# One 128x512 product expands a group of 512 edges in the head and scatter stage: windows of 16 rows for each tile, offsets for four groups in one load

## The chip, the cores and the metric

One core of one Trainium2 chip runs the whole program. The metric is the device time of one launch in microseconds. Lower is better.

## What is computed

Four graph layers run one after the other on 3125 nodes with 128 features and 53125 edges, which are sorted by their destination. Only the third and the fourth matter here. N, D, H, Dh are 3125, 128, 8, 16.

```python
# layer 3 (x, k, q, v: one row for each node)
kw = jnp.einsum('ehd,hdo->eho', k[src], rel_att)
a = jnp.einsum('eho,eho->eh', kw, q[dst]) * rel_pri * inv_sqrt_d
m = jnp.einsum('ehd,hdo->eho', v[src], rel_msg)
attn = softmax of a over the edges of one dst
h_agg = jax.ops.segment_sum(m * attn[..., None], dst, num_segments=N)
...
# layer 4: rows = src, cols = dst
gathered = vals[:, None] * x[cols]
side = jax.ops.segment_sum(gathered, rows, num_segments=n)
```

Layer 3 needs the row q[dst] for each edge, and layer 4 the row x[dst]. Both are got by expansion: since the edges are sorted by dst, a short window of node rows holds all that a group of edges needs, and a product with a matrix of ones and zeros copies each row to its edges. With the inputs of this case the 512 edges of any group span at most 35 nodes, and the 128 edges of any tile at most 11, which was counted from dst.

## The kernel before

Edges are cut into Q = 104 groups of GE = 512, and each group into J = 4 tiles of 128. Every layer makes a pass over the 104 groups. The stage that changes is `head_and_rows`, and it makes two such passes, which overlap by two groups. The head pass (layer 3) works on kv rows gathered by src and on rows of `q_table`. The rows pass (layer 4) works on rows of `x_last`, multiplies them by the edge's weight and scatters them by src order. `number[rows, q]` numbers the 208 expansions of the two passes from 0, and n below is that number.

One expansion takes these steps, each on its own queue:

- **SP** (`load`): reads the group's first node from `base_sb` into a register (L419), loads the offsets of the 512 edges from that node, broadcast to 64 partitions (L2003, 128 KB written, waits for `spread_made` of two expansions ago), and then loads the window, 64 node rows to 64 partitions (L2013, 32 KB, waits for `expanded` of expansion n - 3, since there are WS = 3 window slots).
- **ACT** (`spread_out`): spread = relu(1 - |offset - lane|) in two operations on 64x512 (L2196, L2198). This is the 0/1 matrix. It waits for `expanded` of expansion n - 2.
- **PE** (`expand`): four products of 64 rows, one for each tile of 128 edges, into the 128x512 buffer `ps_q[n % 2]` (L2059). It waits for the window, the spread, and `taken` of expansion n - 2.
- **DVE**: `score` (L2335) in the head pass or `weigh_row` (L2273) in the rows pass takes `ps_q`, and sends `taken`.
- **POOL**: in the head pass, four indirect DMAs for each group gather kv rows (L1971). Group q waits for `expanded` to reach q - 4. In the rows pass, four indirect DMAs for each group scatter the weighed rows (L1985), after `taken` of this group and `expanded` of the next one.

The order on each engine is written out: `turns` gives the turns, and in turn t every engine runs its part of group t, with the softmax of a chunk of 13 groups (`links` on SP: 16 loads, L1995; `maxima`, `sums`, `shares` on DVE), the summing up of the head pass (`total_up`, L2095) and in the rows pass the counting that gives each row its place (`count` on PE, L2072 to L2074; `mark` and `place` on DVE) between the expansions. PE's instructions are executed in that order, so are SP's and ACT's.

The first layer's pass (`rel` tables, L703 to L780) already works by tiles: there the windows of a group are four loads of 64 rows (L722), one for each tile, with the bases of the four tiles read at once (`window_bases`). The set-up of the changed stage on DVE (L2553 to L2565) ends with the semaphore `set_up`, for which ACT waits before its first spread.

Of the kernel before, what the change touches and what calls it, by code (L numbers as in the profile page):

```python
# [26 lines left out]
P = 128  # L27
N = 3125
D = 128
# [37 lines left out]
def build(nc, x, src, dst, edge_attr_64, edge_type_4, edge_weight, node_type_3,  # L67
# [22 lines left out]
    key_row = dram("tile_keys", [Q, GE])  # L90
    type_row = dram("edge_types", [Q, GE])
# [32 lines left out]
    def lay_out(src_t, w_t, near_t, part_t):  # L124
        with ExitStack() as ctx:
# [32 lines left out]
            with nc.Block() as block:  # L158
# [34 lines left out]
                def _(sp):  # L193
# [21 lines left out]
                    sp.dma_start(key_row, key_s[:, :]).then_inc(stored, 16)  # L215
                    sp.wait_ge(near, 1)
# [4 lines left out]
                    sp.wait_ge(stored, 16 * 7)  # L221
# [3 lines left out]
                def _(dve):  # L225
# [62 lines left out]
                    for g in range(NG - 1):  # L288
                        dve.tensor_scalar(late[:, g:g + 1], rows[0:1, 0, READY[g] + 1:READY[g] + 2], float(GN * (g + 1)), float(GE), ALU.is_lt, ALU.mult).then_inc(reached, 1)
                        dve.tensor_scalar(late[:, NG + g:NG + g + 1], rows[0:1, 0, SAFE[g]:SAFE[g] + 1], float(GN * (g + 1) - REACH), float(GE), ALU.is_gt, ALU.mult).then_inc(reached, 1)  # L290
# [117 lines left out]
    def far_spread(eng, program):  # L408

        reach = nc.values_load(wide[0:1, 3:4], engines=[eng.engine], min_val=0, max_val=GE,  # L410
# [1407 lines left out]
    def head_and_rows(agg2, parts, below, bucket, first_bucket, bucket_base):  # L1818

        with ExitStack() as ctx:  # L1820
            tmp, psum, sem, pair = scope(ctx, "e2")
            ROWS = CH * H
            RING, WS = 24, 3
# [7 lines left out]
            offsets, window = tmp("offsets", [P, WS, GE]), tmp("window", [P, WS, D])  # L1831
            spread = tmp("spread", [P, 2, GE])
            minus_lane = tmp("minus_lane", [P, P // WIN])
            a_now, attn = tmp("a_now", [P, 2, J, ROWS]), tmp("attn", [P, 2, CH, J * H])
# [57 lines left out]
            win_in, offsets_in, src_in, sent = pair("win_in", WS), pair("offsets_in", WS), pair("src_in", RING), pair("sent", RING)  # L1892
# [16 lines left out]
            SOFT, JOIN, N_WEIGHTS, SET_UP = 9, 16, 8, 4  # L1909
# [42 lines left out]

            def slot_free(eng, v):
# [11 lines left out]
            def pool_program(pool):  # L1965
# [7 lines left out]
                far_spread(pool, lambda nw, gw, early: send_rows(pool, early))  # L1973
# [16 lines left out]
            def sync_program(sp, nw, gw, early):  # L1990
# [7 lines left out]

                def load(rows, q):
                    n = number[rows, q]  # L2000
                    base = group_base_of(sp.engine, q)
                    hold(sp, spread_made, nw * (n - WS + 1))
                    sp.dma_start(offsets[0:gw, n % WS, :], near_row[q:q + 1, :].broadcast_to([gw, GE])).then_inc(offsets_in[n % WS], 16)  # L2003
                    if rows:
                        if q == 0:
                            sp.wait_ge(pads_stored, 16 * 4)
                        for g in range(NG):
                            if q == (SAFE[g - 1] + 1 if early and g else 0):
                                sp.wait_ge(own_stored[g], 16)
                    for w in range(nw):  # L2010
# [899 lines left out]
```

## Time and profile before

| | us |
|---|---|
| median of 3 runs | 3078.84 (3070.05 to 3078.93) |
| profiled execution, span | 3100.3 |
| head pass, first to last gather issue on POOL | 1672.1 to 2299.5 |
| rows pass, first to last scatter issue on POOL | 2321.6 to 2949.0 |
| busy over the span: PE, PEld | 2081.7, 1679.2 |
| busy over the span: DVE, ACT, POOL | 1578.6, 1176.2, 1685.1 |

Only the span of the profiled execution is known, not a time of its own around it. The span is 21.5 us (0.7%) over the median of the runs that were timed without the profiler. In the page, the share of busy time is an average over layers with different work, PE's time contains matmuls whose ends are modelled, and SP's own work (reading registers and issuing DMAs) is not counted as busy.

### The profile page before, as it was taken

How to read it: one execution, taken by the hardware profiler on the slowest of the kernel's cores; microseconds unless marked ns; L12 is line 12 of the kernel's file. 1: busy time of each engine (PE TensorE's matmuls, PEld its weight loads, DVE VectorE, ACT ScalarE, POOL GpSimd, SP SyncE). 2: the span in 40 equal slices, each digit the busy share in tenths (PEclk: the TensorE clock that was granted, in tenths of full speed). 3: DMA queues.
4: the chain of work that ended last, by engine and by line, in shares of the span. 5: the costliest groups of instructions: out<-in, count | busy, mean ns of one | idle time of the engine just before them, and what ended most of it. 6: DMA issues, size and time to landing. Idle time of an engine off the chain costs nothing. (4 is left out here: it accounts for less than half of the span.)

```text
span 3100.3 us, 39481 instructions
## 1 busy us (share of the span) xinstructions
PE 2081.7 (67%) x9935; PEld 1679.2 (54%) x9935; DVE 1578.6 (51%) x4421; ACT 1176.2 (38%) x3344; POOL 1685.1 (54%) x1704
## 2 busy tenths in 40 slices
PE   5436777777765778788782356767777656555367
PEld 2235666666654667667671355556655433333267
DVE  4246767676751242423232434657688654444356
ACT  1245556555332223233231344445454322222244
POOL 3366656565104565565643666666646666666600
PEclk9655565656567889889986555555567665565589
DMA  6644444444103223232322444444432222222264
GB/s 223 233 139 128 129 114 136 117 126 115 41 19 86 71 67 80 65 80 65 81 64 73 126 119 120 115 125 123 124 98 70 75 69 78 71 71 72 65 242 141
DMA packets 244614, 322.44 MB, mean 104 GB/s; under 512 B 105346, under 2 KB 160931, under 8 KB 243045
## 3 DMA queue, kind: packets, MB, share of 16 engines
q0 software_dynamic: 66560, 163.90, 18.6%
q1 hardware_dynamic: 177797, 155.67, 16.6%
q8 instruction: 93, 1.52, 0.2%
q14 instruction: 164, 1.34, 0.1%
HBM read 257.60 MB, written 63.38 MB: 104 GB/s over the span
## 5 line engine op out<-in xcount | busy, mean ns | idle before, releaser
L1422 POOL DMA_INDIRECT e_gathered<-msg_src_table,src_idx x416 | 396.6, 953 | 420.9 <-issue 269.2
L703 POOL DMA_INDIRECT e_gathered<-rel_src_table,rel_idx x416 | 433.5, 1042 | 300.3 <-issue 245.6
L1971 POOL DMA_INDIRECT e_kv<-kv_table,src_idx x416 | 410.1, 986 | 275.3 <-issue 195.1
L1985 POOL DMA_INDIRECT rows_by_src<-e_kv,e_row x416 | 419.3, 1008 | 230.2 <-issue 202.0
L2059 PE MATMUL e_ps_q<-e_window,e_spread 64*128 64x128 f32 x1664 | 350.9, 378 | 151.8 <-ACT e_spread L2198 63.6
L2059 PEld LDWEIGHTS e_ps_q<-e_window,e_spread 64*128 64x128 f32 x1664 | 306.9, 275 | 223.8 <-issue 210.9
L2196 ACT ACTIVATE e_spread<-e_offsets,e_minus_lane 64x512 f32<-64x512 f32 x208 | 149.1, 717 | 563.6 <-remote 340.3
L764 PE MATMUL e_ps_r<-e_window,e_spread 64*128 64x128 f32 x832 | 201.0, 413 | 159.3 <-DMA e_window<-rel_dst_table 109.4
L2095 PE MATMUL e_ps_a<-e_onehot,e_weighted 128*128 128x128 f32 (+1 forms) x832 | 185.3, 396 | 144.7 <-issue 67.2
L764 PEld LDWEIGHTS e_ps_r<-e_window,e_spread 64*128 64x128 f32 x832 | 172.3, 304 | 185.5 <-DMA e_window<-rel_dst_table 117.4
L2095 PEld LDWEIGHTS e_ps_a<-e_onehot,e_weighted 128*128 128x128 f32 x832 | 166.5, 297 | 170.9 <-issue 99.3
L1685 DVE TENSOR_TENSOR e_shifted<-e_ps_m,e_b 128x512 f32<-128x512 f32 x104 | 71.8, 690 | 354.6 <-PE e_ps_m L1520 199.8
L779 PE MATMUL e_ps_a<-e_typed,e_rel 128*128 128x128 f32 (+1 forms) x832 | 187.9, 400 | 52.9 <-DVE e_typed L1074 20.0
L779 PEld LDWEIGHTS e_ps_a<-e_typed,e_rel 128*128 128x128 f32 x832 | 169.9, 302 | 74.2 <-issue 45.5
L2072 PE MATMUL e_ps_c<-e_inside,e_minus_after 128*128 128x392 f32 x104 | 77.0, 838 | 191.4 <-DVE e_carry L2289 107.4
L1513 PEld LDWEIGHTS e_ps_h<-ident,e_gathered 128*128 128x128 f32 x832 | 128.5, 223 | 83.7 <-issue 56.5
L1529 PE MATMUL e_ps_a<-e_mixed,e_message 128*128 128x64 f32 x832 | 117.0, 288 | 76.3 <-DVE agg L1694 61.0
L1608 ACT ACTIVATE e_hidden<-e_ps_h,e_b 128x512 f32<-128x512 f32 x104 | 71.4, 686 | 245.2 <-remote 99.6
L939 ACT ACTIVATE e_gathered<-e_gathered 128x128 f32<-128x128 f32 x416 | 122.4, 295 | 89.9 <-issue 53.7
L1529 PEld LDWEIGHTS e_ps_a<-e_mixed,e_message 128*128 128x128 f32 x832 | 110.7, 207 | 81.8 <-issue 81.1
L1057 DVE TENSOR_TENSOR e_rel<-e_gathered,e_ps_r 128x512 f32<-128x512 f32 x104 | 70.8, 681 | 163.2 <-DMA e_gathered<-rel_src_table,rel_idx 72.6
L1508 PE MATMUL e_ps_h<-e_rhs,e_lhs 128*128 128x512 f32 x208 | 132.5, 723 | 22.9 <-ACT e_rhs L1603 20.0
(477 smaller groups left out, 4266.0 us busy)
## 6 DMA issues: line engine op xcount, KB each, us to landing
n_rows<-rows_by_src SPq DMA_DIRECT2D x26, 1032.0 KB
e_offsets<-group_offsets SPq DMA_DIRECT2D x208, 128.0 KB
e_keys<-tile_keys SPq DMA_DIRECT2D x104, 128.0 KB
e_window<-rel_dst_table SPq DMA_DIRECT2D x416, 32.0 KB
e_mixed<-in_edge_attr_dram SPq DMA_DIRECT2D x103, 128.0 KB
rel_src_table<-t_up SPq DMA_DIRECT2D x5, 2560.0 KB
e_gathered<-rel_src_table,rel_idx POOLq DMA_INDIRECT x416
e_gathered<-msg_src_table,src_idx POOLq DMA_INDIRECT x416
```

What stands on the lines that cost most here:

```text
L703: pool.indirect_dma_start(gathered[:, q % GS, j, :], None, rel_table, bass.IndirectOffsetOnAxis(ap=rel_idx[:, q * J + j:q * J + j + 1], ax ...
L764: mm = pe.matmul(ps_r[q % 3][:, j, :], spread[:, at % SS, j * P:(j + 1) * P], window[:, at % WS, j, :], start=(w == 0 and (nw == 1 or j == ...
L779: pe.matmul(ps_a[at % 2][:, a:b], rel[:, p % SLOTS, j, :], by_key[:, a:b], start=True, stop=True, skip_group_check=True)
L1422: pool.indirect_dma_start(gathered[:, q % GS, j, :], None, msg_table, bass.IndirectOffsetOnAxis(ap=src_idx[:, q * J + j:q * J + j + 1], ax ...
L1508: pe.matmul(ps_h[q % 2][:, :, :], lhs[0:k, at % WS, :], rhs[0:k, at % 2, :], start=(w == 0), stop=False, skip_group_check=True).then_inc(s ...
L1513: mm = pe.matmul(ps_h[q % 2][:, j, :], gathered[:, q % GS, j, :], ident[:, :], start=False, stop=True, skip_group_check=True)
L1529: mm = pe.matmul(ps_a[:, :], message[:, q % 2, j, :], picked, start=(j == 0), stop=(j == J - 1))
L1971: pool.indirect_dma_start(kv[:, q % RING, j, :], None, kv_table, bass.IndirectOffsetOnAxis(ap=src_idx[:, q * J + j:q * J + j + 1], axis=0) ...
L1985: pool.indirect_dma_start(in_order, bass.IndirectOffsetOnAxis(ap=row[:, q // 2 % RS, q % 2 * J + j:q % 2 * J + j + 1], axis=0), kv[:, slot ...
L2059: mm = pe.matmul(ps_q[n % 2][:, j, :], spread[0:gw, at % 2, j * P:(j + 1) * P], window[0:gw, at % WS, :], start=(w == 0 and (nw == 1 or j ...
L2095: mm = pe.matmul(to[:, 0:n], weighted[:, p % 2, j, :], wide_hot[:, j * (gw + 2):j * (gw + 2) + n], start=(j == 0), stop=(j == J - 1), skip ...
L2196: act.activation(spread[0:gw, at % 2, :], offsets[0:gw, n % WS, :], ACT.Abs, bias=minus_lane[0:gw, w:w + 1]).then_inc(distant, 1)
```

## The change

The stage now expands a group by tiles. Each tile's window has NEAR = 16 node rows. The four windows lie on the diagonal of a 128x512 buffer: tile j's rows in partitions 32j to 32j + 15 and columns 128j to 128j + 127, zeros elsewhere. The buffer is cleared once at the start of the stage. The spread is one 128x128 matrix: partition 32j + i holds a one at edge e when edge e of tile j has offset i from the tile's first node. One product of 128x128 with 128x512 then gives all four tiles. The offsets from a tile's first node are loaded for four groups at once, from a table `tile_offsets` that the layout stage now stores as well. The path of wide spreads keeps the old form, and the branch between the two paths reads `wide[5]` in place of `wide[3]`.

```diff
-            RING, WS = 24, 3
+            RING, WS, OS = 24, 3, 2
-            offsets, window = tmp("offsets", [P, WS, GE]), tmp("window", [P, WS, D])
-            spread = tmp("spread", [P, 2, GE])
+            BATCH = 4
+            offsets, window = tmp("offsets", [P, OS, GE]), tmp("window", [P, WS, J * D])
+            spread = tmp("spread", [P, 2, P])
...
+                def load_offsets(b):
+                    q = b % NBATCH * BATCH
+                    if b >= OS:
+                        sp.wait_ge(spread_made, spread_with(b - OS, early))
+                    for j in range(J):
+                        sp.dma_start(offsets[j * WIN:(j + 1) * WIN, b % OS, :].rearrange("p (g e) -> p g e", e=P),
+                                     lane_row[q:q + BATCH, j * P:(j + 1) * P].rearrange("(a g) e -> a g e", a=1).broadcast_to([WIN, BATCH, P])).then_inc(offsets_in[b % OS], 16)
...
+                    if nw == 1:
+                        if q % BATCH == 0:
+                            load_offsets(batch_of(rows, q))
+                        bases = window_bases([sp.engine], q)
...
+                        hold(sp, expanded, n - WS + 1)
+                        for j in range(J):
+                            sp.dma_start(window[j * WIN:j * WIN + NEAR, n % WS, j * D:(j + 1) * D],
+                                         (x_last if rows else q_window)[bass.ds(bases[j], NEAR), :]).then_inc(win_in[n % WS], 16)
...
+                    if nw == 1:
+                        pe.wait_ge(win_in[n % WS], 16 * J * (n // WS + 1))
+                        pe.wait_ge(spread_made, n + 1)
+                        hold(pe, taken, n - 1)
+                        pe.matmul(ps_q[n % 2][:, :, :].rearrange("p j f -> p (j f)"), spread[:, n % 2, 0:P], window[:, n % WS, :],
+                                  start=True, stop=True).then_inc(expanded, 1)
...
+                        act.activation(spread[:, n % 2, 0:P], offsets[:, b % OS, at:at + P], ACT.Abs, bias=tile_lane[:, 0:1]).then_inc(distant, 1)
+                        act.wait_ge(distant, n + 1)
+                        act.activation(spread[:, n % 2, 0:P], spread[:, n % 2, 0:P], ACT.Relu, bias=1.0, scale=-1.0).then_inc(spread_made, 1)
...
+                dve.tensor_scalar(quarters[:, :], iota[:, WIN:P:WIN], lane[:, 0:1], None, ALU.is_le).then_inc(set_up, 1)
+                dve.memset(window[:, :, :], 0.0).then_inc(cleared, 1)
+                dve.wait_ge(set_up, 3)
+                dve.tensor_reduce(quarter[:, :], quarters[:, :], AX.X, ALU.add).then_inc(set_up, 1)
+                dve.wait_ge(set_up, 4)
+                dve.tensor_scalar(tile_lane[:, :], quarter[:, :], float(WIN), lane[:, 0:1], ALU.mult, ALU.subtract).then_inc(set_up, 1)
...
+                    sp.dma_start(lane_row, dl_s[:, :]).then_inc(stored, 16)
```

SP waits for the clearing of the window buffer before its first load of the stage.

On **SP**, in the middle of the head pass, the queue of two groups stood like this before (a row that says ISA is the arithmetic on a register that holds the address, and L419 reads the base):

```order
L419 TENSOR_LOAD base_sb
L2003 DMA e_offsets<-group_offsets 64x512
L2013 ISA
L2013 DMA e_window<-q_table 64x128
L419 TENSOR_LOAD base_sb
L2003 DMA e_offsets<-group_offsets 64x512
L2013 ISA
L2013 DMA e_window<-q_table 64x128
```

Now one group, the first of a batch of four, takes this:

```order
L2018 DMA e_offsets<-tile_offsets 32x4x128
L2018 DMA e_offsets<-tile_offsets 32x4x128 x3
L120 TENSOR_LOAD base_sb
L2040 ISA
L2040 DMA e_window<-q_table 16x128
L2040 ISA
L2040 DMA e_window<-q_table 16x128
L2040 ISA
L2040 DMA e_window<-q_table 16x128
L2040 ISA
L2040 DMA e_window<-q_table 16x128
```

The other three groups of the batch have the same rows without the two for the offsets. A group issued two DMAs before, and it now issues four, or eight where a batch begins, five in the mean.

On **PE**, in the same place (`e_ps_q` is the expansion, `e_ps_a` the summing up of the head pass), two groups before:

```order
L2059 MATMUL e_ps_q<-e_window,e_spread 128x128 x4
L2095 MATMUL e_ps_a<-e_onehot,e_weighted 128x128 x3
L2095 MATMUL e_ps_a<-e_onehot,e_weighted 128x66
L2059 MATMUL e_ps_q<-e_window,e_spread 128x128 x4
L2095 MATMUL e_ps_a<-e_onehot,e_weighted 128x128 x3
```

and now:

```order
L2090 MATMUL e_ps_q<-e_window,e_spread 128x512
L2136 MATMUL e_ps_a<-e_onehot,e_weighted 128x128 x3
L2136 MATMUL e_ps_a<-e_onehot,e_weighted 128x66
L2090 MATMUL e_ps_q<-e_window,e_spread 128x512
L2136 MATMUL e_ps_a<-e_onehot,e_weighted 128x128 x3
```

Four products with the same number of columns in all became one, and nothing moved between the other steps. POOL's order and DVE's order in the two passes are as before.

## Rows read from the trace of the kernel before

**Rows 1.** Instructions of POOL by line: count, ns min/median/max, first and last start.
```profile
L703 POOL DMA_INDIRECT e_gathered<-rel_src_table,rel_idx x416: 940/946/1862, 107.5 to 796.7; - x139
...
L1422 POOL DMA_INDIRECT e_gathered<-msg_src_table,src_idx x416: 938/944/1582, 934.3 to 1614.2; - x139
...
L1971 POOL DMA_INDIRECT e_kv<-kv_table,src_idx x416: 940/946/1807, 1672.1 to 2299.5; - x139
...
L1985 POOL DMA_INDIRECT rows_by_src<-e_kv,e_row x416: 963/969/1717, 2321.6 to 2949.0; - x139
```

**Rows 2.** Stretches, head and rows pass: us, busy PE, PEld, DVE, ACT, POOL, clock, DMA.
```profile
1672.10:2299.50 627.40, 389.28 (x1586) 336.16 (x1587) 342.67 (x810) 268.88 (x653) 409.10 (x415) 0.52 0.43 122
2321.60:2949.00 627.40, 363.53 (x1297) 242.57 (x1295) 329.25 (x740) 174.57 (x405) 418.35 (x416) 0.63 0.24 72
```

**Rows 3.** Timeline of POOL: start, length, what, idle time before it.
```profile
1712.81 0.94 POOL L1971 DMA_INDIRECT e_kv<-kv_table,src_idx  x1 [6.04 <-remote]
...
1731.55 0.95 POOL L1971 DMA_INDIRECT e_kv<-kv_table,src_idx  x1 [0.30 <-issue]
...
1735.07 0.94 POOL L1971 DMA_INDIRECT e_kv<-kv_table,src_idx  x1 [2.58 <-remote]
...
2295.45 0.94 POOL L1971 DMA_INDIRECT e_kv<-kv_table,src_idx  x1 [2.27 <-issue]
...
2333.94 0.96 POOL L1985 DMA_INDIRECT rows_by_src<-e_kv,e_row  x1 [2.15 <-issue]
...
2919.71 0.97 POOL L1985 DMA_INDIRECT rows_by_src<-e_kv,e_row  x1 [4.01 <-issue]
```

**Rows 4.** Timeline of the other engines around the pause that ends at 1735.07.
```profile
1719.74 5.69 PE L2059 MATMUL e_ps_q<-e_window,e_spread 64*128 64x128 f32 x24 [4.04 <-issue]
...
1734.36 0.69 DVE L2335 TENSOR_TENSOR e_kv<-e_kv,e_ps_q 128x512 f32<-128x512 f32 x1 [11.13 <-remote]
1734.44 0.72 ACT L2196 ACTIVATE e_spread<-e_offsets,e_minus_lane 64x512 f32<-64x512 f32 x1 [9.64 <-remote]
1734.48 0.48 SPq L2013 DMA_DIRECT2D e_window<-q_table  x1
```

**Rows 5.** Groups by form: busy us, mean ns of one, idle before and releasers.
```profile
L2059 PE MATMUL e_ps_q<-e_window,e_spread 64*128 64x128 f32 x1664 | 350.9, 378 | 151.8 <-ACT e_spread L2198 63.6 <-issue 54.1 <-DVE e_kv L2273 16.8
L2059 PEld LDWEIGHTS e_ps_q<-e_window,e_spread 64*128 64x128 f32 x1664 | 306.9, 275 | 223.8 <-issue 210.9 <-DVE e_shift L2550 6.5
...
L2196 ACT ACTIVATE e_spread<-e_offsets,e_minus_lane 64x512 f32<-64x512 f32 x208 | 149.1, 717 | 563.6 <-remote 340.3 <-PE e_ps_q L2059 125.3 <-issue 71.5
...
L2198 ACT ACTIVATE e_spread<-e_spread 64x512 f32<-64x512 f32 x208 | 131.0, 630 | 6.6
...
L939 ACT ACTIVATE e_gathered<-e_gathered 128x128 f32<-128x128 f32 x416 | 122.4, 295 | 89.9 <-issue 53.7 <-DVE e_gathered L1066 36.1
```

**Rows 6.** Timeline of PE at the half clock: an expansion pair, and a 392-column product.
```profile
1770.28 3.78 PE L2059 MATMUL e_ps_q<-e_window,e_spread 64*128 64x128 f32 x16
...
2560.08 1.65 PE L2072 MATMUL e_ps_c<-e_inside,e_minus_after 128*128 128x392 f32 x2 [9.12 <-DVE e_carry L2289]
```

**Rows 7.** Timeline of SP in the first layer's pass and in the head pass.
```profile
405.37 2.79 SPq L722 DMA_DIRECT2D e_window<-rel_dst_table  x4
...
409.22 3.01 SPq L722 DMA_DIRECT2D e_window<-rel_dst_table  x4
...
1809.25 3.46 SPq L1995 DMA_DIRECT2D e_pen_c<-segment_gates  x8
...
1825.90 0.45 SPq L2003 DMA_DIRECT2D e_offsets<-group_offsets  x1
```

**Rows 8.** Timeline: the layout stage's last store (SP), the changed stage's set-up (DVE).
```profile
20.64 0.38 SPq L220 DMA_DIRECT2D segment_links<-same  x1
...
1672.98 3.15 DVE L2555 MEMSET agg<- 128x3712 f32 x1 [0.71 <-issue]
1676.13 0.23 DVE L2556 MEMSET parts<- 128x210 f32 x1
```

More of the change, by code:

```diff
@@ L406, in by_bucket, with tiles_or_far @@
             program(GE // (2 * BUCKET) + 1, False)
-    def far_spread(eng, program):
-        reach = nc.values_load(wide[0:1, 3:4], engines=[eng.engine], min_val=0, max_val=GE,
+    def tiles_or_far(eng, program):
+        reach = nc.values_load(wide[0:1, 5:6], engines=[eng.engine], min_val=0, max_val=J * GE,
                                skip_runtime_bounds_check_because="every node has an edge of its own")
@@ L1951, in count_of, with batch_of, spread_with @@
                 return (t - s0) // 2 if t >= s0 and (t - s0) % 2 == 0 and (t - s0) // 2 < Q // 2 else None
+            def batch_of(rows, q):
+                return NBATCH * rows + q // BATCH
+            def spread_with(b, early):
+                return 1 + numbers(early)[b >= NBATCH, b % NBATCH * BATCH + BATCH - 1]
             def slot_free(eng, v):
@@ L1997, in sync_program @@
                 number = numbers(early)
+                def load_offsets(b):
[5 more added lines that the diff above has]
+                                     lane_row[q:q + BATCH, j * P:(j + 1) * P].rearrange("(a g) e -> a g e", a=1).broadcast_to([WIN, BATCH, P])).then_inc(offsets_in[b % OS], 16)
                 def load(rows, q):
                     n = number[rows, q]
-                    base = group_base_of(sp.engine, q)
-                    hold(sp, spread_made, nw * (n - WS + 1))
-                    sp.dma_start(offsets[0:gw, n % WS, :], near_row[q:q + 1, :].broadcast_to([gw, GE])).then_inc(offsets_in[n % WS], 16)
+                    if nw == 1:
+                        if q % BATCH == 0:
+                            load_offsets(batch_of(rows, q))
+                        bases = window_bases([sp.engine], q)
+                    else:
+                        base = group_base_of(sp.engine, q)
+                        hold(sp, spread_made, nw * (n - OS + 1))
+                        sp.dma_start(offsets[0:gw, n % OS, :], near_row[q:q + 1, :].broadcast_to([gw, GE])).then_inc(offsets_in[n % OS], 16)
                     if rows:
@@ L2012, in load @@
                         hold(sp, expanded, at - WS + 1)
-                        sp.dma_start(window[0:gw, at % WS, :], (x_last if rows else q_window)[bass.ds(base + w * gw, gw), :]).then_inc(win_in[at % WS], 16)
+                        sp.dma_start(far_window[0:gw, at % WS, :], (x_last if rows else q_window)[bass.ds(base + w * gw, gw), :]).then_inc(win_in[at % WS], 16)
                 def weights():
@@ L2058, in expand @@
                         for j in range(J):
-                            mm = pe.matmul(ps_q[n % 2][:, j, :], spread[0:gw, at % 2, j * P:(j + 1) * P], window[0:gw, at % WS, :],
-                                           start=(w == 0 and (nw == 1 or j == 0)), stop=(w == nw - 1), skip_group_check=True)
+                            mm = pe.matmul(ps_q[n % 2][:, j, :], far_spread[0:gw, at % 2, j * P:(j + 1) * P], far_window[0:gw, at % WS, :],
+                                           start=(w == 0 and j == 0), stop=(w == nw - 1), skip_group_check=True)
                         mm.then_inc(expanded, 1)
```

49 lines of the change are left out of this document (31 added, 18 removed).

## The prediction

> **What bounds the kernel now.** I began with the first and last instruction of each group of indirect DMAs on POOL [rows 1], because all four layers make the same 104 steps with four such DMAs each. The passes take 689.2, 679.9, 627.4 and 627.4 us from first to last start, that is 6.7, 6.6, 6.1 and 6.1 us a group. The last two are the two passes of the stage that changes. The reader is to see that they are equal to a tenth of a microsecond, though they do different work: I then read each engine's busy time in the two stretches [rows 2]. The head pass has ACT busy for 268.88 us and the rows pass for 174.57; the DMA engines are busy for 0.43 and 0.24 of the time; PE is at 0.52 and 0.63 of its clock (mostly the 1.2 GHz level). Nothing of this shows in the pace. POOL alone is alike in both, 409.10 and 418.35 us.
>
> The timeline of POOL [rows 3] shows how its pace is made. In a steady stretch one indirect DMA takes 0.95 us and the next follows 0.30 us later. Four of them are 5.0 us, and no group can take less. The rest are pauses: 36 in the head pass, between the one that ends at 1712.81 and the one that ends at 2295.45, and 34 in the rows pass, up to the one that ends at 2919.71. Their sum follows from the stretches: 627.4 - 409.1 - 379 x 0.30 = 105 us in the head pass and 627.4 - 418.35 - 381 x 0.30 = 95 us in the rows pass. So about 200 us of 1255 are pauses of 2.9 us each. This is all that a change of the expansion can win here, since POOL's own DMAs are not touched.
>
> The last view is the timeline of the other engines at one pause [rows 4]. POOL stands still until 1735.07. DVE has stood for 11.13 us and goes on at 1734.36, ACT has stood for 9.64 us and goes on at 1734.44, and SP issues the next window at 1734.48. All four wait for `expanded`, which PE sends. But PE's rows show its three expansions of this place done at 1719.74 + 5.69 = 1725.43, nine microseconds before. The trace names no releaser (it says remote). So in the pauses PE's signal comes late, and the rows do not say why: neither ACT, DVE nor SP had anything to do in the meantime. The reader should take from this that the pauses are real, that they hang on the signal of the expansion, and that their cause does not stand in any row.
>
> **The change part by part.**
>
> *PE.* Each expansion had four products over 128 columns, and now one over 512. The columns are the same. Two expansions, sixteen records (each product is two), take 3.78 us together at the half clock, 1.89 us for one [rows 6]. A product of 392 columns takes 1.65 us in two records, which makes 1.65 x 512 / 392 = 2.15 us for 512 columns with its tail counted in. So PE wins between 0.1 us and nothing: I take 0. The weight loads (306.9 us for 1664 of them [rows 5]) lie beside the matmuls in these rows, or 1.89 us would not be less than 2.15. The Trainium skill says otherwise (TensorE: Matmul & The Clock Gate, on what overlaps and what doesn't, in the part on packing small matmuls): loads overlap matmuls in flight only when they use another row group, and all of these use the same rows. By that rule three of every four loads would have cost PE time and would now be gone, 0.75 x 306.9 = 230 us of PE time. The pitch of the rows speaks against it.
>
> *ACT.* The two operations on 64x512 take 717 and 630 ns [rows 5]; the nearest one on 128x128 takes 295 ns. Two of those are 0.59 us, so each spread is ready 1.347 - 0.59 = 0.76 us sooner, and 208 of them take 157 us off ACT. ACT waited 563.6 us before these operations, so its load did not matter. The 0.76 us lie on the path from one expansion to the one after the next.
>
> *SP.* The nearest rows are those of the first layer's pass, which loads four windows a group: 2.79 and 3.01 us for the four, and 409.22 - 405.37 = 3.85 us from group to group, with one load of keys between them [rows 7]. There the windows have 64 rows, here 16, so this may be too much. The window was one DMA of 0.48 us, and the last of its four parts is now issued 2.8 - 0.5 = 2.3 us later. The offsets were a DMA of 0.45 us a group and are now one a group in the mean. `links` adds 2 x 3.46 us in 13 groups, 0.5 us a group. In all SP needs 3.85 + 0.5 = 4.4 us a group, under the 5.0 us of POOL. It can keep up in the mean, but when SP is released after a pause it now brings a window every 3.9 us, where its two DMAs took 0.48 + 0.45 us [rows 4, 7] beside the reading of the base.
>
> *DMA.* A group loads 64 KB of offsets in place of 128 KB, in rows of 512 bytes in place of 2 KB, and the same 32 KB of window. The two passes have 0.43 and 0.24 of DMA time and the same pace [rows 2], so I take 0 for that. The Trainium skill (DMA: Bandwidth & Descriptors, rules for kernel authors) speaks against this side of the change: it says to coalesce many small transfers, and that below 64 KB one pays mostly overhead. The first layer's pass agrees in part, since it issues four windows of 32 KB a group and is slower by 0.6 us a group, but the second layer's pass is as slow.
>
> *The start of the stage.* DVE now clears 128x1536 before anything else. The clear of 128x3712 took 3.15 us [rows 8], so this is 3.15 x 1536 / 3712 = 1.3 us, and three operations of some 0.2 us each wait for each other. SP's first window waits for the clear, ACT's first spread for the whole set-up, which comes 1.3 + 0.7 = 2.0 us later. Then SP issues eight DMAs before the first expansion in place of two, 6 x 0.65 = 3.9 us, some of it beside the set-up. POOL's first groups do not wait, but from group 5 on it follows the expansions, and its first pause of 6.04 us hangs on them. Bounds: 0 if this is absorbed, 6 us if nothing is; I take 4. The layout stage stores one more table of 208 KB; its last such store takes 0.38 us to issue [rows 8]. I take 0.4 us.
>
> *The pauses.* This is the unknown term. The trace does not show what holds the signal back, so the price of the change there has to be bounded from both sides: below, all 200 us of pauses go; above, every one of the 70 pauses is longer by the 2.3 us of SP, 161 us. I take 0, and the nearest rows for that are the two passes themselves [rows 2]: very different loads on ACT, PE and the DMA queues, and pauses of 105 and 95 us. That no engine's load shows in them is the best evidence that this change's loads won't.
>
> The sum: 0 (PE) + 0 (ACT, hidden) + 0 (DMA) + 4 (start) + 0.4 (layout) + 0 (pauses) = +4 us. Against the profiled span that is 3100.3 + 4 = 3104; against the median of the runs, which lies 21.5 us lower, 3078.84 + 4 = 3083 us. I call 9 us (0.3%) the smallest difference that a measurement of this kernel tells from none.
>
> **The rivals.**
>
> *A, the pauses stay (0.38).* As above, 3083 us. ACT's win is hidden since ACT was idle, PE's columns are the same, POOL's DMAs are the same. By itself this case holds 3070 to 3095: an average pause that changes by a tenth makes 20 us in the sum, so even here a part falls outside the band of 9 us on either side.
>
> *B, the signal comes sooner (0.34).* If the time from one release to the next expansion counts in every pause, each is shorter by ACT's 0.76 us: 70 x 0.76 = 53 us, 3030 us. For it: ACT's spread is the releaser most named for PE's expansions, 63.6 us of their idle time [rows 5]. If more expansions get done in each release, a few pauses of 2.9 us fall away in addition. If PE's weight loads were not hidden after all, the gain would be on the same path and larger: as far as 2880 us with all pauses gone. Against it: DVE and ACT wait for 10 us and more in a pause, for which 0.76 us is small, and the pass with less work for ACT is not faster.
>
> *C, SP brings the windows late (0.26).* A window now has four issues behind each other, and the next group's stand behind those. It decides when two expansions are released together and the slots are empty: the second window is then complete on the queue 3.9 + 2.8 us after the release, where it took 0.93 + 0.48 us and the reading of a base. From the point where the window comes later than the spread and `taken`, PE waits for it, and POOL with it. If half of the 70 pauses grow by 2.3 us, it is 80 us, 3078.84 + 4 + 80 = 3163 us; if a quarter do, 3123. For it: the first layer's pass, with four windows a group, has 6.7 us a group [rows 1], against 6.1 here; 208 x 0.6 = 125 us would be the most. Against it: the second layer's pass loads one window a group and has 6.6.
>
> *D, the wide path is taken (0.02).* The branch now also asks for tiles that span fewer than 16 nodes and for the last node of certain groups. The first layer's pass already takes its near path by a test of the same kind, and the counts from dst (11 nodes in a tile) allow it. If the wide path ran, the time would be hundreds of us more, and I leave it out of the range.
>
> **How the numbers follow.** Case A is the likeliest, so I predict 3083 us. The range has to take in B at 3030 and most of C at 3123: 3015 to 3140, which leaves out the far ends of B and of C, and D. Within 9 us of 3078.84: three quarters of A, 0.28, and a little of B and C, 0.02, in all 0.30. Faster by more than that: most of B and a small part of A, 0.36. Slower: 0.34.
>
> **What would show it right or wrong.** Right, if POOL's two passes again take about 627 us each with some 35 pauses of 3 us. ACT's two operations should fall from 280 us to about 125, and PE's expansion of one group stay near 1.9 us at the half clock. SP should show four windows in 2 to 3 us. B shows as fewer or shorter pauses on POOL at the same 5.0 us a group between them. C shows as PE waiting for the DMA of the window, which no row of this stage has now. The prediction fails if the pauses move with the change at all in one direction, by more than a tenth, since I hold that they don't hang on ACT's, PE's or SP's time. The start is wrong if the first expansion comes over 6 us later after the stage's start than now.

## The result, and the profile after

The changed kernel takes 3102.17 us (median of 10 runs, 3091.70 to 3117.82), the kernel before beside it 3080.07 us (10 runs, 3066.97 to 3090.51). The ratio is 1.0069, with a 95% interval of 1.0052 to 1.0086: some 21 us slower. The forecast of 3083 us was 19 us too low; the time lies in the range, but above the 3070 to 3095 us that case A was to hold by itself, and about halfway between A at 3083 and the lower of C's two times, 3123.

The profiled executions have nearly the same span, 3099.4 us after and 3100.3 before, so the loss can't be read off the spans. The first layer's pass and the second layer's, which the change does not touch, are 3.2 and 12.1 us shorter in this one execution than in [rows 1]. Only the changed stage can be compared, and it is longer: from the first gather to the last scatter 2949.1 - 1658.8 = 1290.3 us, where it was 2949.0 - 1672.1 = 1276.9 us. The page after, its head and the groups that answer to [rows 1, 5]:

```profile
span 3099.4 us, 38862 instructions
...
L2090 PE MATMUL e_ps_q<-e_window,e_spread 128*128 128x512 f32 x416 | 312.4, 849 | 449.7 <-DMA e_window<-x_last 198.4
...
L2238 ACT ACTIVATE e_spread<-e_offsets,e_minus_tile_lane 128x128 f32<-128x128 f32 x208 | 82.6, 397 | 667.2 <-DMA e_offsets<-tile_offsets 278.6
```

The two passes, first gather to last and first scatter to last, in the same columns as [rows 2]:

```profile
1658.80:2280.80 622.00, 299.02 (x976) 178.64 (x976) 338.63 (x798) 201.35 (x640) 411.02 (x415) 0.68 0.40 112
2310.80:2949.10 638.30, 314.18 (x682) 147.09 (x682) 328.67 (x740) 110.96 (x403) 421.61 (x416) 0.73 0.21 61
```

Every engine has less to do than before or nearly the same, PE by 139 us in the two passes together (613 against 753) and ACT by 131 us, and the stage is no shorter. PE's part is not less work: its granted clock in the two passes was 0.52 and 0.63 before and is 0.68 and 0.73 after, and busy time times clock, an estimate of the work, is 431 us before and 433 after. What is new is who is waited for. For PE's line of the expansion after (matmuls and weight loads together), its instructions and what ended its idle time:

```profile
L2090 PE MATMUL e_ps_q<-e_window,e_spread x416: 590/697/1223, 1666.8 to 2938.3; 128*128 128x512 f32 x139
...
  DMA e_window<-x_last: 437.1, 79
  DMA e_window<-q_table: 409.4, 76
  issue: 144.5, 102
```

846 us in 155 waits for a window's transfer, where no row of this line had named the window as a releaser. The sum has most waits twice, once before the weight load and once before the matmul: of it, 390.3 us in 76 waits are the matmuls' own (198.4, shown in the page's row, and 191.9). The sums of this view below, 783 and 160 us, count both in the same way. These waits are the sign that the prediction gave for rival C. The waits of POOL, before and then after (us in total, times, longest us), show how much of it arrives at the engine that sets the pace:

```profile
POOL rows_by_src L1985 <- issue: 202.0, 401, 4.3
POOL e_kv L1971 <- issue: 195.1, 403, 3.7
...
POOL rows_by_src L1985 <- DVE e_row L2301: 22.0, 4, 21.1
POOL e_kv L1971 <- remote: 21.3, 6, 6.0
...
POOL rows_by_src L1985 <- PE e_ps_q L2059: 1.0, 1, 1.0
```

```profile
POOL rows_by_src L1999 <- issue: 206.8, 405, 7.1
POOL e_kv L1985 <- issue: 183.3, 405, 3.8
...
POOL rows_by_src L1999 <- DVE e_row L2351: 29.0, 1, 29.0
POOL e_kv L1985 <- PE e_ps_q L2090: 27.1, 8, 11.2
POOL rows_by_src L1999 <- PE e_ps_q L2090: 8.1, 4, 4.5
```

Waits for the expansion grew from 1.0 to 35.2 us, and the unnamed ones (remote) fell from 21.3 to none. The waits for DVE's row grew by 7.0, nearly all of it one event between the passes (21.1 before, 29.0 after); "issue" fell by 7.0. The longest new wait can be followed from engine to engine, at the start of the stage; SP first:

```profile
1663.05 19.54 SPq L2040 DMA_DIRECT2D e_window<-q_table  x12
1683.28 10.50 SPq L2009 DMA_DIRECT2D e_pen_c<-segment_gates  x8
1694.49 9.09 SPq L2009 DMA_DIRECT2D e_same_c<-segment_links  x8
1703.69 1.84 SPq L2040 DMA_DIRECT2D e_window<-q_table  x4
```

```profile
1706.89 2.08 PE L2090 MATMUL e_ps_q<-e_window,e_spread 128*128 128x512 f32 x2 [21.79 <-DMA e_window<-q_table]
```

```profile
1709.72 0.95 POOL L1985 DMA_INDIRECT e_kv<-kv_table,src_idx  x1 [11.16 <-PE e_ps_q L2090]
```

SP needs 19.54 us for the windows of three groups and 20 us for `links`. The fourth group's window is issued at 1703.69, PE expands at 1706.89, and POOL has stood for 11.16 us. In [rows 7] the eight DMAs of one half of `links` took 3.46 us; here they take 10.50 and 9.09. The kernel before was slow at this place too, with 7.38 and 7.07 us for the same two halves, but by then it had issued its first three windows within 4.1 us of its first DMA.

And this is not only the start. Two pieces of SP's timeline in the rows pass, a few microseconds apart, with the windows of four groups each:

```profile
2591.16 29.76 SPq L2040 DMA_DIRECT2D e_window<-x_last  x16
2621.61 1.01 SPq L2018 DMA_DIRECT2D e_offsets<-tile_offsets  x4
2623.13 8.92 SPq L2040 DMA_DIRECT2D e_window<-x_last  x16
```

The same instructions take 29.76 us and then 8.92, and four groups last 24 us. SP's instructions by kind (ns min/median/max) say what stretches them:

```profile
L2040 SPq FUSED_REGOPS  x832: 1/37/1407, 1662.9 to 2935.2; - x167
L2040 SPq MOVE e_window<-q_table x416: 1/29/716, 1663.0 to 2299.0; - x139
L2040 SPq DMA_DIRECT2D e_window<-q_table x416: 1/316/1407, 1663.0 to 2299.1; - x139
```

A register operation that takes 37 ns in the median takes up to 1407 ns. Three of four wait for nothing, the one of 1407 ns at 2610.37 among them, so it is not the transfer that is slow. In such stretches SP's instructions, one by one, come in steps of some 0.70 us, whatever they do. A group's four windows, from the start of the first DMA to the end of the last, take 2.2 us in the median of the 208 groups, 3.7 in the mean, over 5.0 in 53 groups and 11.2 at most. Each window needs three (two register instructions for its address, and the DMA), and a group needs one load of the bases more: 13.

From this came theory S: SP's instructions, too many for the stretches in which each takes 0.70 us, bring windows late. Its rivals were D, that the number of small transfers does; P, that the cost sits with the product, the spread or the offsets; and, for the offsets alone, O.

### The profile page after: what moved, and what is told of

Its sections match the earlier page's. It is cut to its first block and busy times, and to the rows that moved or that the text cites. A ratio compares the mean times of both kernels' runs of the same rounds, so it can differ in the third digit from the quotient of the medians.

```text
span 3099.4 us, 38862 instructions
## 1 busy us (share of the span) xinstructions
PE 1940.5 (63%) x8687; PEld 1424.7 (46%) x8687; DVE 1580.1 (51%) x4425; ACT 1046.1 (34%) x3344; POOL 1691.5 (55%) x1704
## 3 DMA queue, kind: packets, MB, share of 16 engines
q8 instruction: 82, 1.34, 0.2%
## 5 line engine op out<-in xcount | busy, mean ns | idle before, releaser
L2090 PE MATMUL e_ps_q<-e_window,e_spread 128*128 128x512 f32 x416 | 312.4, 849 | 449.7 <-DMA e_window<-x_last 198.4
L2090 PEld LDWEIGHTS e_ps_q<-e_window,e_spread 128*128 128x128 f32 x416 | 90.0, 253 | 552.9 <-DMA e_window<-x_last 238.7
L2238 ACT ACTIVATE e_spread<-e_offsets,e_minus_tile_lane 128x128 f32<-128x128 f32 x208 | 82.6, 397 | 667.2 <-DMA e_offsets<-tile_offsets 278.6
L2136 PEld LDWEIGHTS e_ps_a<-e_onehot,e_weighted 128*128 128x128 f32 x832 | 144.2, 252 | 206.8 <-issue 105.6
L2136 PE MATMUL e_ps_a<-e_onehot,e_weighted 128*128 128x128 f32 (+1 forms) x832 | 146.6, 336 | 116.2 <-DVE e_weighted L2394 62.8
L2323 DVE TENSOR_TENSOR e_kv<-e_ps_q,w_t 128x512 f32<-128x512 f32 x104 | 71.5, 688 | 173.9 <-PE e_ps_q L2090 107.5
L2253 ACT ACTIVATE e_onehot<-marks,part_t 128x66 f32<-128x66 f32 x416 | 110.3, 336 | 140.6 <-remote 73.8
```

What stands on the lines that cost most here:

```text
L2090: pe.matmul(ps_q[n % 2][:, :, :].rearrange("p j f -> p (j f)"), spread[:, n % 2, 0:P], window[:, n % WS, :], start=True, stop=True).then_i ...
L2136: mm = pe.matmul(to[:, 0:n], weighted[:, p % 2, j, :], wide_hot[:, j * (gw + 2):j * (gw + 2) + n], start=(j == 0), stop=(j == J - 1), skip ...
```

## The experiments

The jobs fell under two kinds of condition, and no result can be read without this. In one kind the kernel before takes 3078 to 3084 us, as in the times given at first; in the other 2747 to 2751 us. All runs of a job were of one kind, except two single runs of 4147 and 3189 us in 2750 jobs that fit neither, and the kernel before ran beside each. The kind does not belong to a chip: one chip had both, at different times. I call them **the 3080 kind** and **the 2750 kind**.

**1. Windows from fixed rows.** SP issues the same transfers with 1872 instructions fewer, 9 for each of 208 expansions.

```
-  bases = window_bases([sp.engine], q)
-  (x_last if rows else q_window)[bass.ds(bases[j], NEAR), :]
+  (x_last if rows else q_window)[30 * q + 7 * j:30 * q + 7 * j + NEAR, :]
```

> The changed kernel, but each window is read from a row number fixed in the program, not from the tile's own base: SyncE keeps its four window transfers per group and loses the load of the bases and the two register instructions ahead of each transfer (13 instructions per group become 4). The expansions so compute with wrong rows; every size and wait is the same. Theory S (SyncE's instruction stream is what brings windows late: in the trace of the changed kernel many of its instructions stand 0.70 us apart in stretches, e.g. 8 windows in 18.4 us): the stretches get rare, TensorE's idle time before the expansion for the window's transfer falls from 846 us (437 + 409) to under 400, and the time falls from 3102 to 3070 to 3085. Rival D (the number of small transfers itself, or their landing, is what costs): 3095 to 3105, and the idle time stays near 850. Rival P (the cost sits with the product, the spread or the offsets): 3095 to 3105, whatever SyncE does.

Measured: 2748.46 us against 2748.68, ratio 0.9997 (0.9986 to 1.0009). The job was of the 2750 kind, which no theory had foreseen.

**2. Two windows of four from ACT's queue.**

```
-  for j in range(J):
+  for j in range(2):
...
+  def act_windows(rows, q):
+      bases = window_bases([act.engine], q)
...
+      hold(act, expanded, n - WS + 1)
+      for j in range(2, J):
+          act.dma_start(window[j * WIN:j * WIN + NEAR, n % WS, j * D:(j + 1) * D], ...
```

> The changed kernel with two of the four windows of a group issued from ScalarE's queue, ahead of the spread of the same group, the other two from SyncE's. Same transfers, same number of slots; ScalarE gets 7 more instructions per group. Theory S: two instruction streams bring the windows in time, 3080 to 3092, with less idle time of TensorE for the window. Rival D (number of transfers): no change, 3095 to 3105. Rival A (ScalarE, which waits for the offsets and for the product before it, then brings its windows late instead): 3105 to 3130, and TensorE's idle time for windows rises.

Measured: ratio 0.9981 (0.9967 to 0.9995), 2742.55 us.

**3. Five slots.**

```
-  RING, WS, OS = 24, 3, 2
+  RING, WS, OS = 23, 5, 2
```

> The changed kernel with five slots for windows in place of three (and 23 in place of 24 slots for the gathered rows, to make room): SyncE may run four groups ahead of the product and not two. Theory S in the form that SyncE is late only in bursts of 10 to 20 us: the extra 12 us of lead cover most of them, 3080 to 3092, and TensorE's idle time for windows falls from 846 us to under 500. If SyncE is late on average (11 to 15 instructions of 0.70 us are 8 to 10 us per group against 6 us that a group takes), more slots bring nothing: 3097 to 3105. Rival P: 3097 to 3105, with idle time moved from the window to another release.

Measured: ratio 0.9990 (0.9977 to 1.0002), 2746.70 us. Its trace serves below as the changed kernel in the 2750 kind, since the change itself, with nothing else altered, had no job there.

**4. The kernel before with SP's and the DMA queues' share of the change.**

```
-  base = group_base_of(sp.engine, q)
+  bases = window_bases([sp.engine], q) if nw == 1 else None
+  base = bases[0] if nw == 1 else group_base_of(sp.engine, q)
...
+  for j in range(1, J):
+      sp.dma_start(window[48 + NEAR * j:64 + NEAR * j, n % WS, :],
+                   (x_last if rows else q_window)[bass.ds(bases[j], NEAR), :]).then_inc(win_in[n % WS], 16)
...
-  pe.wait_ge(win_in[at % WS], 16 * (at // WS + 1))
+  pe.wait_ge(win_in[at % WS], 16 * (J if nw == 1 else 1) * (at // WS + 1))
```

> The kernel before, with its one product form and its wide spread, plus three more windows of 16 rows per group at the tiles' bases, put in unused partitions of the window's slot; TensorE's first product waits for all four transfers. Nothing reads the three. This adds to the kernel before SyncE's instructions and transfers of the change and none of its arithmetic. Theory S and rival D: all of the loss or more is there, 3100 to 3115 (5 transfers and 15 to 17 instructions per group), with rows in which TensorE waits for the window's transfer. Rival P: 3077 to 3085, no change against the kernel before.

Measured: ratio 0.9997 (0.9987 to 1.0008), 2747.34 us. SP has 3066 instructions in the stage here and 3067 in the change, so SP's load is matched. All four kernels are the same as the kernel before within 0.2%. The trace of the third shows what is missing in this kind. POOL's waits, PE's waits at the expansion, and SP's instructions by kind:

```profile
POOL e_kv L1985 <- issue: 122.6, 402, 0.3
...
POOL rows_by_src L1999 <- issue: 118.0, 387, 0.3
...
POOL rows_by_src L1999 <- PE e_ps_q L2090: 6.2, 7, 4.4
```

```profile
  DMA e_window<-q_table: 76.8, 16
  DVE e_kv L2385: 55.4, 34
...
  DMA e_window<-x_last: 0.9, 1
```

```profile
L2040 SPq FUSED_REGOPS  x832: 37/37/47, 1508.0 to 2537.0; - x167
L2040 SPq MOVE e_window<-q_table x416: 29/29/39, 1508.1 to 2017.9; - x139
```

The longest "issue" of POOL is 0.3 us: within the two passes there is not one pause between its DMAs (the 4.4 us stand between the passes), and they take 536.5 and 548.9 us, 5.2 and 5.3 us a group. No register operation of SP takes over 47 ns. So the pauses of this stage, 200 us of which the prediction took for a property of this kernel, and the stretches of SP both belong to the 3080 kind. Where they are missing, the passes run within 0.3 us of POOL's 5.0 us a group, and SP's three further windows are hidden. That left open whether the loss itself needs the 3080 kind.

**5. The change again.**

> The changed kernel as it is, beside the kernel before, on the chip that this job gets. The four experiments before this ran on a chip on which the kernel before takes 2748.7 us, not 3080, and on which POOL's two passes of the stage have no pause at all. Theory H (the loss of 21 us exists only where a chip has the pauses of 3 us and the stretches of SyncE instructions 0.70 us apart; without them SyncE's five transfers per group are hidden): if the kernel before takes about 2750 here, the change takes 2742 to 2754, a ratio of 0.997 to 1.002; if it takes about 3080, the change takes 3095 to 3110. Rival (the loss is a property of the program): 1.005 to 1.008 on either chip.

Measured: the job was of the 3080 kind, 3101.42 us against 3077.94, ratio 1.0072 (1.0048 to 1.0097). The loss is repeated, inside the 3095 to 3110 us of theory H. Experiment 3, the nearest kernel in the 2750 kind, has no such loss, so it very likely belongs to the 3080 kind. PE waited 399.9 + 383.4 = 783 us for windows (weight loads and matmuls together, 361 us of it the matmuls' own), and POOL 37.4 us for the expansion.

**6 to 9. Experiments 1, 4 and 2 for the 3080 kind, and the offsets a batch ahead.** The last loads each batch of offsets four groups sooner:

```
-  RING, WS, OS = 24, 3, 2
+  RING, WS, OS = 23, 3, 3
...
-  load_offsets(batch_of(rows, q))
+  b = batch_of(rows, q)
+  if b == 0:
+      load_offsets(0)
+  if b + 1 < 2 * NBATCH:
+      load_offsets(b + 1)
```

> The kernel of the first experiment again (windows from fixed rows, 4 SyncE instructions per group in place of 13; it computes with wrong rows), now wanted beside a kernel before of about 3078 us. Theory S (the number of SyncE's instructions makes windows late, since in stretches one takes 0.70 us): TensorE's idle time for the window's transfer falls from 783 us (400 + 383) to under 300 and the time is 3065 to 3085, a ratio of 0.996 to 1.002. Rival D (it is the number of small transfers in flight): the ratio stays at 1.005 to 1.009 with the idle time near 780. If the kernel before takes about 2750 here, all four runs of this job give 0.997 to 1.002.

> The kernel of the fourth experiment again (the kernel before plus three unused windows of 16 rows per group and TensorE waiting for them). Theory S: the loss or more is there, ratio 1.005 to 1.012, with TensorE waiting for the window's transfer, since SyncE has 15 to 17 instructions per group. Rival P (the loss sits with the product, the narrow spread or the offsets of four groups): 0.998 to 1.002.

> The kernel of the second experiment again (two windows of a group from ScalarE's queue, two from SyncE's). Theory S: SyncE has 9 instructions per group in place of 13, and ScalarE has time; ratio 0.997 to 1.004, better than the 1.007 of the change. Rival A (ScalarE's instructions are as slow and its windows late): 1.007 to 1.02.

> The changed kernel with three slots for offsets in place of two, and each batch of offsets for four groups loaded four groups earlier (23 slots for gathered rows make room). ScalarE's idle time of 309 us for the offsets' transfer should fall under 50. Theory S: the windows stay late and the time stays, ratio 1.005 to 1.009, with TensorE's idle time for the window at 700 to 850 us. Rival O (the offsets, which stand ahead of the windows in SyncE's queue, are what comes late, and the spread with them): 0.999 to 1.003.

Measured: the job was of the 2750 kind. Ratios 0.9995 (0.9981 to 1.0009), 1.0003 (0.9987 to 1.0019), 1.0006 (0.9989 to 1.0023) and 0.9997 (0.9983 to 1.0011). None tells S from a rival. They do bound the arithmetic: with windows in time, the changed kernel with its offsets loaded earlier (0.9997) is the same as the kernel before within 0.2%.

**10. Fixed rows, once more.**

> The changed kernel with each window read from a row fixed in the program (4 SyncE instructions per group in place of 13, the same four transfers; it computes with wrong rows), once more, for a chip on which the kernel before takes about 3078 us. There, theory S (the number of SyncE's instructions makes windows late) says: ratio 0.996 to 1.002 and TensorE's idle time for the window under 300 us, not 783. Rival D (the number of small transfers) and rival P (product, spread, offsets) say: ratio 1.005 to 1.009. On a chip with about 2748 us all say 0.998 to 1.002.

Measured: the job was of the 3080 kind, 3041.72 us (5 runs, 3036.63 to 3047.51) against 3084.23, ratio 0.9872 (0.9849 to 0.9895). D and P are out as causes of the loss: the four small transfers a group, the product, the spread and the offsets are all still there, and SP now has as many instructions in the stage as in the kernel before (1195 and 1194). Theory S is right in its direction and in the idle time (160 us, under 300), but the time is below its range of 0.996 to 1.002: more was won than the loss, and S does not say why. The edit takes three things away at once, the reading of the bases, the register instructions, and addresses from registers in the transfers; the rows read are also others. The run does not part these. The trace, PE's waits at the expansion and then SP's windows by kind:

```profile
  DMA e_window<-q_table: 156.1, 28
  DVE e_kv L2322: 11.8, 4
  DMA e_window<-x_last: 4.1, 4
```

```profile
L2039 SPq DMA_DIRECT2D e_window<-q_table x416: 3/420/1397, 1660.9 to 2275.4; - x139
```

The waits for windows fell from 783 to 160 us, and the matmuls' own from 361 to 73 us. The stretches are still there, a DMA still takes up to 1397 ns, but four instructions a group get through them sooner: no group's four windows take over 5.0 us (the longest 4.91), where 53 of 208 did. At the start of the stage, against 19.54 us for the first twelve windows of the change:

```profile
1660.86 5.57 SPq L2039 DMA_DIRECT2D e_window<-q_table  x12
```

And POOL's waits:

```profile
POOL e_kv L1985 <- issue: 187.0, 409, 6.3
POOL rows_by_src L1999 <- issue: 172.0, 410, 4.6
...
POOL rows_by_src L1999 <- DVE e_row L2350: 23.6, 1, 23.6
POOL e_kv L1985 <- remote: 8.5, 1, 8.5
POOL rows_by_src L1999 <- PE e_ps_q L2089: 4.9, 1, 4.9
```

From experiment 5 to this one the stage went from 1286.6 to 1227.3 us. Of these 59 us, 32.5 are POOL's waits for the expansion (37.4 to 4.9), 25.6 are "issue" (384.6 to 359.0, the unnamed pauses), 10.6 are POOL's own DMAs (840.3 to 829.7 us), and 8.5 came back as "remote".

**11 and 12. Two windows from ACT's queue, twice more.**

> The changed kernel with two windows of a group from ScalarE's queue and two from SyncE's, a version that computes the reference, once more for a chip on which the kernel before takes about 3080 us. There windows from fixed rows (4 instructions per group) gave a ratio of 0.987, the change (13 instructions) 1.007. Theory S, linear in SyncE's instructions: with 8 per group about 0.996, 0.990 to 1.001, and TensorE's idle time for windows between 160 and 783 us, about 400. Rival A (ScalarE runs short of instructions just as SyncE does, and all that was saved returns there, or in front of the spread): 1.004 to 1.015.

> The kernel of the run before this one again (two windows of a group from ScalarE's queue), since that run had a kernel before of 2751 us, where the change costs nothing. Beside a kernel before of about 3080 us theory S says a ratio of 0.990 to 1.001 with TensorE's idle time for windows at 160 to 783 us, about 400; rival A says 1.004 to 1.015.

Measured: both jobs were of the 2750 kind, ratios 0.9987 (0.9974 to 1.0001) and 0.9998 (0.9980 to 1.0016). With experiments 2 and 8 there are four such results, from 0.9981 to 1.0006; only the interval of the first leaves 1 out, and the other three did not repeat it. What it does in the 3080 kind wasn't seen, and neither was experiment 4 there, the run that would have put SP's load alone into the kernel before. No version that does the whole work is shown here to beat the kernel before.

## Why the prediction was right and wrong

The time fell into the range, but that was luck as far as the mechanism goes: the sum's +4 us had SP and the pauses at nothing, and the loss came through SP. The range reached up to 3140 only to take in rival C.

**PE, 0: held.** At the half clock a product of 512 columns takes 2.08 us alone, where one expansion alone took 2.04 and two together 3.78 us [rows 6], and in experiment 10 the new product costs nothing that shows. The prediction weighed a rule of the Trainium skill (TensorE: Matmul & The Clock Gate, what overlaps and what doesn't) by which three of four weight loads would have given PE time back. PE's busy time did fall, by 139 us in the stage, but times the granted clock it is the same, 431 and 433 us, so the rows show no PE time that the loads had cost; why the clock rose is not shown. In the 2750 kind experiments 3 and 4, with the one product and with four, are equal too, 0.9990 and 0.9997. The rows speak against the rule here, as the prediction had it.

**ACT, 0: size off, place right.** The two operations take 397 and 309 ns, 147 us in all, not the 125 that came from the nearest row. Its 0.64 us of lead per spread did not show by itself. ACT then waited 278.6 us for offsets, a wait that the sum did not have. Experiment 9 loaded them earlier only in the 2750 kind, so its share stays open. Experiment 10 kept the same loads and batches, and there the wait for offsets was 39.3 us; but waits without a releaser (remote) rose from 34.0 to 228.4 us, and ACT's whole idle time before the spread fell only from 667 to 554 us. So part of that wait came from what stood in SP's queue, and how much of it cost time is not shown.

**DMA, 0: held.** Experiment 10 has all four small transfers of a group and is faster than the kernel before. The Trainium skill (DMA: Bandwidth & Descriptors, rules for kernel authors) advises to coalesce small transfers, since below 64 KB one pays mostly overhead. The runs do not show that price here, with 8 KB a transfer: what the four transfers cost was SP's instructions ahead of them.

**SP, "In all SP needs 3.85 + 0.5 = 4.4 us a group, under the 5.0 us of POOL": the step that failed.** It used 2.79 and 3.01 us for four windows [rows 7], from the first layer's pass. The same view of the same stretch has others, which I had left aside:

```profile
312.19 5.25 SPq L722 DMA_DIRECT2D e_window<-rel_dst_table  x4
...
343.11 6.79 SPq L722 DMA_DIRECT2D e_window<-rel_dst_table  x4
...
378.38 6.58 SPq L722 DMA_DIRECT2D e_window<-rel_dst_table  x4
```

Four windows take from 2.45 to 6.79 us in that stretch, and over the whole first pass 3.0 in the median, 3.7 in the mean and over 5.0 in 25 of 104 groups. With 5.25 to 6.79 us in place of 2.79, the sum's 4.4 us a group becomes 6.8 to 8.4 us, against the 6.1 us that a group lasts, and the windows come late where a slow stretch lasts longer than the two groups of lead, as the 29.76 us from 2591.16 do. The prediction's sign, "four windows in 2 to 3 us", is there in the median (2.2) and missing in a quarter of the groups. The prediction read one price where the rows have two, and called the mean of a queue "under" a bound while its spread went over it. Take the 9 instructions a group away, with the bases that they read, and 1.0072 becomes 0.9872: more than the loss.

**The pauses, 0, and rival C.** The mechanism of C was right, and its size came from the wrong place. C let 18 to 35 pauses grow by 2.3 us each. They did not grow: above 0.5 us there are 62 gaps in the two passes after and 70 before, and those without a named releaser (issue and remote) are 56 of 2.9 us in the mean against 68 of 2.8. Their sum fell from 192 to 160 us, a sixth, so by the prediction's own sign ("by more than a tenth") its claim that the pauses do not hang on SP's, PE's or ACT's time failed. What came instead were 12 waits of POOL for the expansion, 35.2 us in all, the longest 11.2, while 21.3 us of unnamed waits went. The stage is longer by 13.4 us in this trace: 34.2 from the waits for the expansion, 7.0 from those for DVE's row and 5.2 from POOL's own DMAs, less 21.3 (remote), 7.0 (issue) and some 4.7 in small waits. In the trace of experiment 5 it is longer by 9.7. Both are of the order of the 21 us between the medians; the traced executions can't fix it closer, since untouched passes differ by as much as 12 us. What decides, by these rows, is not the 2.3 us of one window but how long a slow stretch lasts.

**Rival B.** The prediction gave B 3030 us, if a sooner spread also shortened the pauses. Experiment 10 took 3041.72, 42 us under the kernel before, with fewer pauses: 45 gaps above 0.5 us. So it may be that the gain of B is in the change and SP's cost of some 60 us lies on top of it. The runs do not show this. Against the kernel before, experiment 10 has the same number of SP instructions, 5 a group, but also half the bytes of offsets, no reading of a base and no register instruction, and none of these was tried alone in the 3080 kind.

**The start, +4.** The first expansion comes 1666.75 - 1658.78 = 7.97 us after the first gather, before it was 1678.71 - 1672.07 = 6.64. The clear took 1.34 us, as estimated, and DVE's set-up hides the rest: +1.3 us, not 4. The price of the start came later, with the fourth window behind `links`, as a wait of 11.16 us on POOL where the first pause was 6.04 us [rows 3].

**The chances.** "That no engine's load shows in them is the best evidence that this change's loads won't" was the reason for the case at 3083 us. The pauses do need the 3080 kind, since in the 2750 kind neither the changed form (experiment 3) nor the old one (experiment 4) has any in its two passes. But within the 3080 kind they moved with SP's instructions: 62 gaps above 0.5 us in the change, 60 in experiment 5 and 45 in experiment 10. And SP itself is slowed in the same kind of condition. The sign of C was to be a wait "which no row of this stage has now", when the rows of the first layer's pass already had it: PE waited there 109.4 us in 27 waits for windows of `rel_dst_table`.

## What to carry to other kernels

Price a queue's work by the spread of its rows, not by the fastest of them, and compare it with the bound for as long as a slow stretch lasts. When one transfer is split in four at addresses from registers, count the instructions and not only the DMAs: here they went from 5 a group to 14, and taking the nine away won back more than the loss with all four transfers in place. And where a pause has no releaser in the trace, test first whether it belongs to the program at all: a variant that wins or loses only under one kind of condition wants its ratio from jobs of that kind, beside the kernel before.

## What the runs showed of the hardware

**One program has two times, job by job.** The kernel before takes 3078 to 3084 us in some jobs and 2747 to 2751 us in others, some 12% apart. TensorE's granted clock over the whole run read lower in the 3080 kind, 0.66 to 0.69 against 0.69 to 0.71; whether that is cause or effect is not shown. POOL is not slower: one gather takes the same in both, here in the change (3080 kind) and in experiment 3 (2750 kind):

```profile
L1985 POOL DMA_INDIRECT e_kv<-kv_table,src_idx x416: 943/949/2002, 1658.8 to 2280.8; - x139
```

```profile
L1985 POOL DMA_INDIRECT e_kv<-kv_table,src_idx x416: 942/947/1833, 1502.8 to 2039.3; - x139
```

The Trainium skill (Advanced Engine Details and Errata, clock domains) tells of power profiles; at its profile 2 every measured sequencer and semaphore cost reads 1.18 to 1.25 times that of profile 0. The rows speak against that here, since medians of POOL's DMAs (949 and 947 ns) and of SP's register operations (37 and 37 ns) are equal. The difference lies in stretches: pauses of some 3 us on POOL, and instructions of SP that take 700 or 1400 ns in place of 37.

**SP's stretches do not depend on what the instruction does.** Register operations, moves and DMA issues are slowed alike (in the change up to 1407, 716 and 1407 ns in the rows above). In experiment 3 the first two never take over 47 and 39 ns; a window's DMA takes over 600 ns in 13 of 832 issues there and in 154 of 832 in the change. That looks like instructions that arrive late. But the traces' own transfers of instructions are as many in both, 274, and as long: the large ones of 16 KB have medians of 995 ns in the change and 1040 in experiment 3. No run here shows where SP's instructions wait, and this stays open, as does what sets the kind of a job.
